# Two windowed attention stacks on one Trainium2 core: weights turned on VectorE, V stationary, O written transposed

## What is computed

```python
DEPTH, HEADS, DIM_HEAD, WINDOW = 6, 16, 64, 32
def local_attention(q, k, v):          # q, k, v: b, 16 heads, n, 64
    # windows of 32 rows; a window's queries see the window before and their own
    bk2, bv2 = look(bk), look(bv)      # 64 keys, 64 values to a window
    sim = einsum('bhwie,bhwje->bhwij', bq, bk2) * 8.0
    attn = softmax(where(mask, -max, sim), -1)
    return einsum('bhwij,bhwje->bhwie', attn, bv2)
for i in range(DEPTH):
    x = attn_layer(shift_tokens(x), ...) + x     # qkv product, l2norm, rotary, local_attention, @ Wo
    x = ffn_layer(shift_tokens(x), ...) + x      # layernorm, W1, a * gelu(gate), W2
```

## Time and profile before

| | us |
|---|---|
| median of 3 runs | 4426.52 (4419.78 to 4433.16) |
| the profiled execution, its own time | 4439.44 |
| its span | 4438.1 |
| PE busy | 3859.1 (87%) |
| DVE busy | 3062.1 (69%) |
| POOL busy | 2649.1 (60%) |
| ACT busy | 2568.4 (58%) |

### The profile page before, as it was taken

How to read it: one execution, slowest core, us unless ns; L and a number is a source line. 1 busy time by engine, 2 the same in 40 slices (tenths; PEclk the granted TensorE clock), 3 DMA queues, 4 the chain that set the end, 5 groups by cost and what they waited for, 6 DMA issues and landing times. The chain is left out here.

```text
span 4438.1 us, 158857 instructions
## 1 busy us (share of the span) xinstructions
PE 3859.1 (87%) x66864; PEld 2706.7 (61%) x66864; DVE 3062.1 (69%) x6301; ACT 2568.4 (58%) x4921; POOL 2649.1 (60%) x2218
## 2 busy tenths in 40 slices
PE   7968694399999999999999623999999999999996
PEld 5645453266667666676676422676666676766764
DVE  4446464678777777777777347777777777777773
ACT  3325251266666676666676401666667676666664
POOL 2029074477667676676776203776766767767662
PEclk7569797699999999999999855999999999999998
DMA  0010100133332333333322101333323333233222
GB/s 15 1 33 1 35 1 5 45 93 78 83 85 70 90 80 82 81 82 78 83 65 71 45 7 35 93 82 81 91 65 90 80 85 85 73 87 83 64 71 55
DMA packets 307779, 280.48 MB, mean 63 GB/s; under 512 B 158840, under 2 KB 205696, under 8 KB 307072
## 3 DMA queue, kind: packets, MB, share of 16 engines
q1 hardware_dynamic: 307072, 270.33, 23.9%
HBM read 55.22 MB, written 1.05 MB: 13 GB/s over the span
## 5 line engine op out<-in xcount | busy, mean ns | idle before, releaser
L1459 ACT ACTIVATE m_sq<-PS 128x512 f32<-128x512 f32 x384 | 226.2, 595 | 197.6 <-PE PS L1312 160.8
L1459 ACT ACTIVATE l_sq<-PS 128x512 f32<-128x512 f32 x384 | 226.2, 595 | 196.5 <-PE PS L1312 160.1
L1724 POOL TENSOR_TENSOR l_Pm<-l_Pm,l_rs 128x1024 f32<-128x1024 f32 x96 | 182.9, 1905 | 238.2 <-DVE l_rs L1596 238.2
L1724 POOL TENSOR_TENSOR m_Pm<-m_Pm,m_rs 128x1024 f32<-128x1024 f32 x96 | 182.9, 1905 | 233.7 <-DVE m_rs L1596 233.7
L124 POOL TENSOR_TENSOR rstd<-rstd,minus_half 128x4 f32<-128x4 f32 x40 | 41.9, 1046 | 378.5 <-DVE rstd L120 378.5
L1614 DVE TENSOR_TENSOR XN<-PS,XN 128x128 f32<-128x128 f32 x192 | 56.2, 293 | 279.4 <-PE PS L1364 279.3
L1583 DVE TENSOR_TENSOR l_QR<-PS,l_rot 128x512 f32<-128x512 f32 x192 | 131.8, 687 | 163.2 <-ACT l_sq L1459 163.2
L1583 DVE TENSOR_TENSOR m_QR<-PS,m_rot 128x512 f32<-128x512 f32 x192 | 131.8, 686 | 163.0 <-ACT m_sq L1459 163.0
L1719 POOL TENSOR_TENSOR m_QR<-m_QR,m_UQ 128x1024 f32<-128x1024 f32 x96 | 227.7, 2372 | 24.0 <-DVE m_UQ L1586 24.0
L1719 POOL TENSOR_TENSOR l_QR<-l_QR,l_UQ 128x1024 f32<-128x1024 f32 x96 | 227.7, 2372 | 23.3 <-DVE l_UQ L1586 23.3
L1719 POOL TENSOR_TENSOR l_KR<-l_KR,l_UK 128x1024 f32<-128x1024 f32 x96 | 227.0, 2364 | 0.2 <-DVE l_UK L1586 0.2
(11 more groups left out here) (388 smaller groups left out, 11840.8 us busy)
## 6 DMA issues: line engine op xcount, KB each, us to landing
l_V<-l_Vt SPq DMA_DIRECT2D x576, 128.0 KB
m_V<-m_Vt SPq DMA_DIRECT2D x576, 128.0 KB
l_V<-l_Vt SPq DMA_DIRECT2D x384, 64.0 KB
m_V<-m_Vt SPq DMA_DIRECT2D x384, 64.0 KB
l_wqkv<-l_wqkv_dram SPq DMA_DIRECT2D x72, 128.0 KB, 2.4
m_wqkv<-l_wqkv_dram SPq DMA_DIRECT2D x72, 128.0 KB, 2.5
l_rot<-l_rot_dram SPq DMA_DIRECT2D x24, 256.0 KB, 3.8
m_rot<-l_rot_dram SPq DMA_DIRECT2D x24, 256.0 KB, 3.8
```

The costliest lines, as they stand in the source:

```text
L1459: ac.activation(sq[:, c, b * 512:(b + 1) * 512], PS[:, 2 * c + b, :], ACT.Square).then_inc(sq_out)
L1724: gp.tensor_tensor(pm, pm, over(rs[:, :], 2, [P, 16, 2 * LW]), ALU.mult).then_inc(pn_out)
```

## The change

Within `local_stack` only:

- DVE turns the normalised weights of a tile in 32 x 32 blocks in one instruction (`turn_weights`, `Wt`), at the start of the next step. PE's 8 turns of the weights and ACT's two copies to `pT` are gone.
- V stays in `Vt` as ACT copied it, and a second copy `Vs` is moved on by 32 rows, with two DMAs instead of ten (`shift_v`). Both are double-buffered.
- `values` has V stationary (32 rows x 64 columns) and the turned weights moving (32 rows x 32 columns), adds the window before (`Vs`, k = 0) and the own one (`Vt`, k = 1) in PSUM, and goes over all four 32-row groups, each writing its own bank 4 + w. That is 128 products of 32 rows where 64 of 64 rows were. O comes out transposed, so ACT's two copies make `oT` at once; PE's 8 turns of O and ACT's two copies to `O` are gone.
- The order is written anew: `values(s - 1)` comes after `project_v(s)` and waits for the softmax of tile s, because banks 4 and 5 are shared; `output` moves to the next step, after `project_q`, into bank 7; the feed-forward stages and x's turn use bank 6 and come one to three steps later; the loop has three more rounds at its end.

```diff
@@ pe
+                        te.wait_ge(wT_out, n + 1)
+                        te.wait_ge(V_out, n + 1)
+                        te.wait_ge(v_shift, 32 * (n + 1))
+                        te.wait_ge(ms_out, 2 * min(n + 2, NL))
...
-                            for w in range(4):
-                                for r in range(2):
-                                    m = te.matmul(PS[LW * w:LW * (w + 1), 6 + r, c * LD:(c + 1) * LD],
-                                                  pT[64 * r:64 * r + 64, c, LW * w:LW * (w + 1)],
-                                                  V2[64 * r:64 * r + 64, w, c, :], start=True, stop=True, skip_group_check=True)
+                            for k, V in ((0, Vs), (1, Vt)):
+                                for w in range(4):
+                                    rows = slice(LW * w, LW * (w + 1))
+                                    for r in range(2):
+                                        m = te.matmul(PS[64 * r:64 * r + 64, 4 + w, c * LW:(c + 1) * LW],
+                                                      V[rows, n % 2, r * 512 + c * LD:r * 512 + (c + 1) * LD],
+                                                      Wt[rows, c, r, k, :], start=(k == 0), stop=(k == 1), skip_group_check=True)
@@ act
                     def values_out(n):
                         ac.wait_ge(val_mm, n + 1)
-                        at_ge(ac, ot_turn, 2 * n)
-                        for r in range(2):
-                            ac.copy(O[:, :, r, :], PS[:, 6 + r, :].rearrange("p (c d) -> p c d", d=LD)).then_inc(ov_out)
-
-                    def output_turned(n):
+                        at_ge(ac, out_pr, n)
                         for b in range(2):
-                            ac.wait_ge(ot_turn, 2 * n + b + 1)
-                            at_ge(ac, out_pr, n)
-                            ac.copy(oT[:, 4 * b:4 * b + 4, :].rearrange("p c q -> p (c q)"), PS[:, 6 + b, :]).then_inc(ot_out)
+                            half = slice(4 * b, 4 * b + 4)
+                            ac.copy(oT[:, half, :].rearrange("p c (w i) -> p c w i", w=4),
+                                    PS[:, 4:8, 128 * b:128 * b + 128].rearrange("p w (c i) -> p c w i", i=LW)).then_inc(ot_out)
@@ dve
+                    def turn_weights(n):
+                        ve.wait_ge(pn_out, n + 1)
+                        at_ge(ve, val_mm, n)
+                        ve.transpose(Wt[:, :, :, :, :].rearrange("p c r k i -> p (c r k i)"),
+                                     Pm[:, n % 2, :, :, :].rearrange("p c r k -> p (c r k)")).then_inc(wT_out)
@@ transfers
+                    def shift_v(n):
+                        sp.wait_ge(V_out, n + 1)
+                        at_ge(sp, val_mm, n - 1)
+                        sp.dma_start(Vs[LW:P, n % 2, :], Vt[0:P - LW, n % 2, :]).then_inc(v_shift, 16)
+                        sp.dma_start(Vs[0:LW, n % 2, :], Vt[P - LW:P, (n - 1) % 2, :]).then_inc(v_shift, 16)
```

More of the change, by code:

```diff
@@ L1395, in turn_x @@
                     def turn_x(g):
[L1396 removed]
+                        to_bank(6, [Y[:, 4 * g + j, :] for j in range(4)]).then_inc(x_turn)
                     for g in range(NG):
@@ L1416, in pe @@
                         if 1 <= s <= NL:
-                            output_turn(s - 1)
+                            values(s - 1)
+                        if 0 <= s + 1 < NL:
+                            turn_k(s + 1)
+                            turn_q(s + 1)
+                        if normed is not None:
+                            norm_turn4(s, normed)
                         if widened is not None:
-                            norm_turn4(s, widened)
+                            for c in range(3):
+                                up(s, widened, c)
                         if narrowed is not None:
@@ L1556, in act @@
                                 ac.preload_act_table_set("natural_log_exp_and_others")
+                        if xT is not None and xT < FG - NG:
+                            copy_x(xT + NG, xT % NG)
                 def dve():
@@ L1656, in dve @@
                         norm_apply(g, X, group(Y, g), turned=False)
-                    for s in range(-2, 4 * FG + 8):
-                        widened, narrowed, measured = phase(s, 6), phase(s, 7), phase(s, 5)
+                    for s in range(-2, 4 * FG + 11):
+                        measured, normed, widened, added = phase(s, 6), phase(s, 7), phase(s, 8), phase(s, 10)
+                        if 1 <= s <= NL:
+                            turn_weights(s - 1)
+                        if normed is not None:
+                            middle(normed)
                         if s + 2 < NL:
                             rotate(s + 2, 0)
-                        if widened is not None:
-                            middle(widened)
+                        if added is not None:
+                            down_add(added)
+                        if 2 <= s <= NL + 1:
+                            output_add(s - 2)
                         if 0 <= s < NL:
@@ L1818, in transfers @@
                     load_ffn(0)
-                    for s in range(-2, 4 * FG + 8):
-                        if 0 <= s < NL:
-                            spread_v(s)
-                        done = phase(s, 4)
+                    for s in range(-2, 4 * FG + 11):
+                        done = phase(s, 5)
                         if done is not None:
                             shift(done)
+                        if 0 <= s < NL:
+                            shift_v(s)
                         l, i = layer(s) + 1, s % NT
```

140 lines of the change are left out of this document (44 added, 96 removed).

## The result

The changed kernel takes 5125.37 us (median of 4 runs, 5107.42 to 5139.86), the kernel before 4423.15 us in the runs beside it. The ratio is 1.158, 95% interval 1.154 to 1.162. The forecast of slower held; the size did not: I had said 4635 us, 4450 to 4830, and the loss is 702 us where I had 209.

The account below looks back on a forecast made before the run. PE was taken as the bound. A mean step of 14.06 us plus 4.1 for values made 18.16 against 17.07, +1.09; times 192 steps, +209 us, so 4635 us, range 4450 to 4830.

Parts of the forecast that it names:

- The packet and its wait: In values: 512 small instructions in a row wait about 2 us for a packet in nearly every step, making values 4.1 us.
- my upper end of 5.4: For values: 4.0 us of packet arrival plus 1.41 us of pairs, with nothing fetched ahead.
- The 0.6 us that I took off: In values: average reduction because PE's sequencer may have passed the first packet boundary during V's projection.
- rival 3: Worse: values takes 5.4 us, or longer idle stretches let PE's clock fall; 4885 us, chance 0.12.
- ACT's copies: At the step's end: PE waits 1.6 us in a plain step for ACT to copy oT, K and Q; none after down.
- DVE: The turn of the weights adds 1.2 us, so DVE works 14.2 us a step, still under a step and free beside PE.
- V transfers, turns, new order: Per step of PE: waits for V's transfers go, and turns of weights and O, 1.75 us, go.
- Rival 1: In values: packets come early enough, so values takes 2.4 us; 4310 us, chance 0.12.

Follow-up runs that it names:

- e1: Changed kernel with the half of the values products that adds the window before (k = 0) left out, 128 pairs instead of 256: 4282.67 us.
- e8: Changed kernel with V, its moved copy and the turned weights in bfloat16, 256 small instructions instead of 512: 4276.66 us, ratio 0.963.
- e5: Changed kernel with each small product of values moving 64 columns instead of 32, same instruction count and order: 5032.23 us.
- e3: Changed kernel with four unused products of 256 columns put between the two halves of values: 4992.31 us.
- e4: Changed kernel with four unused products of 256 columns put behind values, ahead of the turn of K: 5470.17 us.
- f1: Changed kernel with values in two halves, the turns of K and Q between them, and ACT copying K and Q ahead of oT: 4849.59 us.
- f2: Changed kernel with values halved, turns of K and Q and the output product between, feed-forward and x's turn in bank 2, output_add last on DVE: 4906.86 us.
- e6: Kernel before, its values made to wait also for the softmax of the next tile, no product added: 4824.89 us.
- e10: Kernel before, the projection of q made to wait for POOL's scaling of K in three of four steps: 5162.05 us.

## Why the prediction was wrong, point by point

- **The packet and its wait: right in kind, 0.8 us short.** I put `values` at 4.1 us with some 2 us of wait in nearly every step. It waits in each of 69 steps, 1.85 us in the mean of the stretch, and is 4.88 us from start to start, between my 4.1 and my upper end of 5.4. The pairs go at today's pace: without its wait `values` takes 3.0 us, 2.9 where the clock is full, and not 2.4. The 0.6 us that I took off because the sequencer might have run ahead is not seen. Of the two statements of the Trainium skill, that a small product has a fixed cost holds, at 10 ns and not at its 60 cycles; that the crossing to the next block of instructions is mostly hidden (Runtime: NRT & Kernel Launch, Instruction fetch mechanics) does not hold for 512 small instructions in a row, 1.85 us a time.
- **The clock: the step that failed.** I had it in rival 3, as one of two reasons, without a price of its own and with a chance of 0.12 for both. It is not an odd event but comes with the wait in most steps: turns of K and Q with what follows at 3.97 us instead of the 2.9 that my sum held (1.74 and a mean wait of 1.2), q and the feed-forward stages 0.4 more. Net of the ACT wait that the slow turns cover, that is 1.4 us a step. The clock itself bears this out: 20% of the time at the half level is 4.1 us a step, which costs at most 2.05.
- **The row was there before.** My reading of the clock stopped at the page's digits outside the stacks and the stretch's 1.00. The same trace of the kernel before, PE's timeline some 8 us behind the earlier trace rows, has it:

```profile
1516.04 1.48 PE L1334 MATMUL PS<-l_V,l_pT 64*32 64x64 f32 x128 [2.54 <-DMA l_V<-l_Vt]
1517.45 3.68 PE L1318 MATMUL PS<-l_wqkv,XNT 128*128 128x512 f32 x4
```

  V's projection takes 3.68 us where the earlier trace rows has 1.98, straight after an idle time of 2.54 us and a run of small products. Having forecast an idle time of 2 us beside even more small products in each step, I should have given what stands behind it at 1.2 GHz a price. How often it would happen, the trace of before did not tell: behind all five waits of 2.5 us or more ahead of `values` in its two stacks the clock fell, but behind those of 1.5 to 2.25 us only once in ten, and here is one where it held:

```profile
1446.68 1.48 PE L1334 MATMUL PS<-l_V,l_pT 64*32 64x64 f32 x128 [1.77 <-DMA l_V<-l_Vt]
1448.10 1.98 PE L1318 MATMUL PS<-l_wqkv,XNT 128*128 128x512 f32 x4
```

  With a fall in every step the price is this. The turns of K and Q are then 3.5 us instead of 1.74, which just hides ACT's 3.3 us of copies: 18.7 us a step, and with 4.9 for `values` 19.5, which gives about 4900 us. The rest is in the turns of x and of the norm, q, `up` and `down`, which the half clock reaches too, and in the second stack. The Trainium skill (TensorE: Matmul & The Clock Gate, HAM oscillation) describes such a pattern, a loop whose every round idles and starts slow again; the trace of the changed kernel agrees in kind, in 62 of 69 steps, but after idle times of 1.85 us where the page's are waits for a DMA of about 3 to 5 us. I did not draw on it.
- **ACT's copies: the wait is real but hidden.** I had 1.2 us a step in the mean; 0.35 is seen, since slow turns take the time that the copies need. e1 and e8, at full clock, show what I should have had with a shorter `values`: 0.78 us a step in e1. The term was 0.4 high even there.
- **DVE: right.** 1.23 us a turn, busy 965 us in 69 steps, 14.0 a step (forecast 14.2).
- **V transfers, turns, new order: right.** No wait for the transfers; 1.76 us of turns gone; k and V now free of what those waits had cost them.
- **Rival 1 was decided by the count, not by the pages.** With `values` at 256 instructions its time is met: e1 and e8 stand at 4283 and 4277, where rival 1 had 4310.

By steps: forecast 18.16. Add 0.8 for `values`, 1.4 for the clock net of the ACT wait it covers, and take off 0.1 for k: 20.3, as measured in the first stack. That 3.2 us more than before, times 192, gives 610 of the 684 us by which the profiled runs differ; 60 more come from the second stack's longer steps. e1, e5 and e8 show a longer step in the second stack as well (16.3, 20.4 and 16.2 us), before does not (16.9); why is open.

## What to carry to other kernels

Before a product is cut into smaller ones, count instructions in a row, not columns: here 256 small ones were nearly free (0.16 us a step) and 512 cost 2 us of waiting in every round, and a longer product between the halves hid most of it (e3) while the same product behind them did not (e4). Pulling the halves apart, each with as many instructions as a packet holds, was not enough (f1, f2). An idle time of TensorE is to be priced with what stands behind it at 1.2 GHz, from a row of the trace where that already happened; look for a product of known length that is suddenly twice as long. Work that keeps an engine waiting elsewhere may be covered by the very slowness one wants to remove, so expect the next wait (here ACT's copies, then DVE) to come up when it is removed.

## What the runs showed of the hardware

- A pair of weight load and matmul of 32 or 64 rows takes 10.0 ns in a run (128 in 1.41 us to the start of what follows), whether it loads 64 columns and moves 32 (e1) or loads 32 and moves 64 (before); 10.9 ns where it loads 64 and moves 64 (e5).
- A packet of the instruction queue is 16 KB, about 250 TensorE instructions (702 packets for 2 x 88368 in the changed kernel). Two start no less than 3.3 us apart (before) or 3.4 (changed kernel), and a waiting TensorE goes on 1.2 to 1.7 us after one has landed (all 69 waits in `values` in the changed kernel's stretch).
- TensorE's clock fell to 1.2 GHz after 1.8 us of idle time in a run of small products (changed kernel), and held at 2.4 GHz after 1.23 us (e6). After waits of 1.5 to 2.25 us in `values` it fell in 57 of 62 cases where 32 columns were moved (changed kernel, clock 0.90) and in 32 of 56 where 64 were (e5, 0.95); in the kernel before, once in ten such waits ahead of `values`.
- It falls also where only long products stand around the idle time: 3.63 us for a product of 1.88 after 5.54 us (e10).
- DVE turns 128 x 1024 values in 32 x 32 blocks in 1.23 us in float32, and in bfloat16 too (e8): half the bytes, the same time.
